# Routed expert blocks with eight row buffers and one plain slice; output weights prepared by GpSimd inside the attention core

## The reference

```
x = x + 0.5 * moe(layernorm(x))        # 16 experts, top 4 by sigmoid(x @ gate) + bias, plus a shared expert
x = x + attention(layernorm(x))        # 32 heads, 8 key/value heads of 16, rotary positions, causal
x = x + 0.5 * moe(layernorm(x))        # the same weights again
x = x + 0.5 * butterfly(layernorm(x))  # permuted features, 16 heads of 32 -> 128 -> 32, gelu
x = x + attention4(layernorm(x))       # 4 sequences, full attention at width 128
x = x + 0.5 * butterfly(layernorm(x))

moe:       zw_e = silu(x @ Wg_e.T) * (x @ Wu_e.T) * cw_e      # 256 columns each
           out  = sum over e of zw_e @ Wd_e.T
attention: out  = softmax(mask(q @ k.T / 16)) @ v @ w_dense.T + b_dense
```

## Time and profile before

| | us |
|---|---|
| median of three runs | 1367.78 (1367.69 to 1369.11) |
| the profiled execution | 1367.37 |
| its span, first to last instruction | 1365.6 |
| TensorE busy | 1144.0 (84%) |
| VectorE busy | 837.1 (61%) |
| ScalarE busy | 665.5 (49%) |
| GpSimd busy | 537.6 (39%) |
| mean granted TensorE clock | 0.905 of full speed |

### The profile page before, as it was taken

One profiled execution on the slowest core, in us unless ns is written; L12 is line 12 of the kernel. 1 busy time (PEld: TensorE's weight loads), 2 busy tenths in 40 slices (PEclk: granted clock), 3 DMA queues, 4 the chain that ended last, 5 costly groups with the idle time before them and its releaser, 6 DMA issues. The chain is left out here.

```text
span 1365.6 us, 22222 instructions
## 1 busy us (share of the span) xinstructions
PE 1144.0 (84%) x5800; PEld 723.2 (53%) x5801; DVE 837.1 (61%) x1527; ACT 665.5 (49%) x1218; POOL 537.6 (39%) x578
## 2 busy tenths in 40 slices
PE   5979999996284899999985796999999808777687
PEld 4747677674173344444424584676776605465454
DVE  4857777773455787777722565777777524445542
ACT  3136666663232277777772222666666503334133
POOL 4325555553673233333324324455555442050130
PEclk9979999998587699999998797999999957979879
DMA  9256989555405440000001454689955550010001
GB/s 349 100 203 156 241 238 248 100 104 90 183 35 133 95 89 2 1 1 1 1 1 39 181 189 170 179 206 264 253 107 100 81 167 0 4 37 0 20 12 62
DMA packets 63497, 151.64 MB, mean 111 GB/s; under 512 B 12560, under 2 KB 17488, under 8 KB 58832
## 3 DMA queue, kind: packets, MB, share of 16 engines
q1 hardware_dynamic: 40224, 99.83, 21.4%
q0 software_dynamic: 22592, 50.27, 19.4%
q10 hardware_dynamic: 624, 0.85, 0.4%
HBM read 105.75 MB, written 44.97 MB: 110 GB/s over the span
## 5 line engine op out<-in xcount | busy, mean ns | idle before, releaser
L715 POOL DMA_INDIRECT moe_acc_rows<-moe_out_rows,moe_token_of x94 | 165.4, 1760 | 196.5 <-ACT moe_out_rows L790 190.4
L1782 DVE TENSOR_REDUCE causal_top<-causal_mx 128x1 f32<-128x512 f32 (+3 forms) x384 | 192.0, 550 | 58.6 <-PE causal_mx L1634 50.5
L1746 ACT ACTIVATE causal_prob<-causal_sc 128x512 f32<-128x512 f32 (+3 forms) x384 | 169.9, 492 | 73.2 <-PE causal_sc L1652 70.7
L819 DVE TENSOR_TENSOR moe_w_lo<-moe_raw,moe_w_hi 128x1024 fp32r<-128x1024 f32 x94 | 115.1, 1225 | 112.7 <-ACT moe_w_hi L778 99.6
L730 PE MATMUL moe_gu<-moe_raw,moe_xt_plain 128*128 x376 | 180.5, 603 | 2.4 <-ACT moe_w_hi L778 2.4
L1631 PE MATMUL causal_mx<-causal_ks,causal_qs 96*128 (+4 forms) x384 | 130.9, 351 | 19.2 <-DMA causal_qs<-causal_parts 15.7
L778 ACT CAST moe_w_hi<-moe_raw 128x1024 fp32r x94 | 98.2, 1045 | 95.2 <-issue 90.8
L1652 PE MATMUL causal_sc<-causal_qs,causal_ks 99*128 (+3 forms) x384 | 123.7, 333 | 2.3 <-ACT causal_prob L1746 1.7
L708 POOL DMA_INDIRECT moe_rows<-moe_xn_rows,moe_token_of x94 | 93.3, 992 | 75.2 <-DVE moe_z L828 31.8
L822 DVE TENSOR_TENSOR moe_down_lo<-moe_raw,moe_down_hi 128x1024 fp32r<-128x1024 f32 x94 | 114.5, 1218 | 0.0
L735 PE MATMUL moe_gu<-moe_w_hi,xt_hi 128*128 128x512 f32 x188 | 112.7, 600 | 0.0
(11 more groups left out here) (273 smaller groups left out, 2425.0 us busy)
## 6 DMA issues: line engine op xcount, KB each, us to landing
moe_raw<-in_w_gu SPq DMA_DIRECT2D x34, 1024.0 KB
moe_raw<-in_w_down SPq DMA_DIRECT2D x34, 512.0 KB
causal_qs<-causal_parts SPq DMA_DIRECT2D x42, 128.0 KB, 3.3
moe_acc_rows<-moe_zeros SPq DMA_DIRECT2D x2, 2304.0 KB, 15.2
moe_acc_rows<-x SPq DMA_DIRECT2D x18, 256.0 KB, 2.0
moe_xn_rows<-xn SPq DMA_DIRECT2D x2, 2048.0 KB, 10.9
x<-moe_acc_rows SPq DMA_DIRECT2D x16, 256.0 KB, 5.3
xn<-moe_acc_rows SPq DMA_DIRECT2D x16, 256.0 KB, 5.9
```

Of the source, the lines that this page charges most:

```text
L715: pool.indirect_dma_start(acc_rows[a], bass.IndirectOffsetOnAxis(ap=token_of[:, b - 3:b - 2].bitcast(U32), axis=0), out_rows[(b - 3) % OUT ...
L819: nc.vector.tensor_tensor(w_lo[1 - s][:, :, :], raw[:, bass.ds(at + SPLIT_AT, GU_COLS - SPLIT_AT)].rearrange("p (k n) -> p k n", k=SPLIT), ...
L1746: nc.scalar.activation(prob[u % 2][:, h, o:CH], sc[(u * QPK + h) % BANKS][:, o:CH], ACT.Exp, scale=SCALE).then_inc(exp_done, 1)
L1782: nc.vector.tensor_reduce(top[:, kc, t, h:h + 1], mx[i % BANKS][:, 0:w], AX.X, ALU.max).then_inc(mx_read, 1)
```

## The change

Three things change in the routed blocks. RING becomes 8 and a new constant AHEAD = 6: the gather of block b+6 is issued in step b, once z of block b-2 is done (for the buffer that it reuses). PLAIN becomes 1, and so SPLIT 3. `out_rows` are slices of `xn`, which frees the space. The loop body of `run` thereby has eight steps.

In the causal attention layer the rounding and subtraction of `w_dense` and the addition of the bias move from the third part into the core, on GpSimd alone, one tile of each per group behind the mask of step 7; `w_dense` comes in two halves. The third part then has no loads and no GpSimd work, and TensorE alternates transposes and products.

```diff
-RING = 4
+RING = 8
+AHEAD = 6
-PLAIN = 2
+PLAIN = 1
 SPLIT = KT - PLAIN
...
-        out_rows = [sb(f"out_rows{s}", [P, H]) for s in range(OUTS)]
+        out_rows = [m.xn[:, s, :] for s in range(OUTS)]
...
-            for b in range(-3, NB + 3):
-                if there(b + 3):
-                    if b > 0:
-                        pool.wait_ge(z_done, b)
-                    pool.indirect_dma_start(rows[(b + 3) % RING][:, :], None, xn_rows, bass.IndirectOffsetOnAxis(
-                        ap=token_of[:, b + 3:b + 4].bitcast(U32), axis=0)).then_inc(gathered[(b + 3) % RING], 16)
+            for b in range(-AHEAD, NB + 3):
+                n = b + AHEAD
+                if there(n):
+                    if n >= RING:
+                        pool.wait_ge(z_done, n - RING + 1)
+                    pool.indirect_dma_start(rows[n % RING][:, :], None, xn_rows, bass.IndirectOffsetOnAxis(
+                        ap=token_of[:, n:n + 1].bitcast(U32), axis=0)).then_inc(gathered[n % RING], 16)
...
+            wd_hi = outer.enter_context(nc.sbuf_tensor(f"{name}_wd_hi", [P, KT, H], F32R))
+            wd_lo = outer.enter_context(nc.sbuf_tensor(f"{name}_wd_lo", [P, KT, H], F32R))
+            wd_raw = sb("wd_raw", [P, KT // 2, H])
+            b_out = sb("b_out", [P, H])
...
                         sp.dma_start(ks[a * HD:(a + 1) * HD, 0:S], parts_dram[K_PART[a], 0:HD, :]).then_inc(stack_in, 16)
+                    sp.dma_start(wd_raw[:, :, :], m.dram["w_dense"][:, 0:KT // 2, :]).then_inc(dense_in, 16)
+                    sp.dma_start(b_out[:, :], m.dram["b_dense"].rearrange("(a h) -> a h", a=1).broadcast_to([P, H])).then_inc(dense_in, 16)
                     with sp.Fori(1, KV) as g:
                         sp.wait_ge(stack_in, g * (16 * LOADS) - 16 * LOADS // 2)
                         load(g)
+                    sp.wait_ge(wd_ready, KT // 2)
+                    sp.dma_start(wd_raw[:, :, :], m.dram["w_dense"][:, KT // 2:KT, :]).then_inc(dense_in, 16)
...
+                    def prepare_dense(g):
+
+                        if g == 0:
+                            pool.wait_ge(dense_in, 32)
+                        if g == KT // 2:
+                            pool.wait_ge(dense_in, 48)
+                        if g < KT:
+                            raw = wd_raw[:, g % (KT // 2), :]
+                            nc.gpsimd.tensor_copy(wd_hi[:, g, :], raw).then_inc(wd_half, 1)
+                            pool.wait_ge(wd_half, g + 1)
+                            nc.gpsimd.tensor_tensor(wd_lo[:, g, :], raw, wd_hi[:, g, :].bitcast(F32),
+                                                    ALU.subtract).then_inc(wd_ready, 1)
+                        nc.gpsimd.tensor_tensor(m.x[:, g, :], m.x[:, g, :], b_out[:, :], ALU.add).then_inc(x_biased, 1)
+
...
+                            if u == C0 + 3:
+                                prepare_dense(g)
...
                 @block.tensor
                 def _(pe):
-                    for t in range(T):
-                        transpose_tile(m, pe, cm, xp[t % 2], t, ready=False)
-                    pe.wait_ge(wd_ready, 1)
-                    for t in range(T):
-                        pe.wait_ge(cm.xt_lo, t + 1)
-                        if t >= 2:
-                            pe.wait_ge(x_done, t - 1)
-                        rows = slice(t * P, (t + 1) * P)
-                        product(nc, yp[t % 2][:, :], [(m.xt_hi[:, k, rows], m.xt_lo[:, k, rows], wd_hi[:, k, :], wd_lo[:, k, :])
-                                                      for k in range(KT)]).then_inc(y_done, 1)
+                    pe.wait_ge(wd_ready, KT)
+                    for t in range(T + 1):
+                        if t < T:
+                            transpose_tile(m, pe, cm, xp[t % 2], t, ready=False)
+                        if t >= 1:
+                            pe.wait_ge(cm.xt_lo, t)
+                            if t >= 3:
+                                pe.wait_ge(x_done, t - 2)
+                            rows = slice((t - 1) * P, t * P)
+                            product(nc, yp[(t - 1) % 2][:, :], [(m.xt_hi[:, k, rows], m.xt_lo[:, k, rows], wd_hi[:, k, :],
+                                                                 wd_lo[:, k, :]) for k in range(KT)]).then_inc(y_done, 1)
...
                 @block.vector
                 def _(dve):
-                    for t in range(T):
-                        lo_tile(m, dve, cm, xp[t % 2], t)
-                    dve.wait_ge(x_biased, 1)
-                    for t in range(T):
+                    def finish(t):
                         dve.wait_ge(y_done, t + 1)
                         nc.vector.tensor_tensor(m.x[:, t, :], yp[t % 2][:, :], m.x[:, t, :], ALU.add).then_inc(x_done, 1)
                         next_stats(m, dve, x_done, t + 1, t)
 
+                    dve.wait_ge(x_biased, T)
+                    for t in range(T):
+                        lo_tile(m, dve, cm, xp[t % 2], t)
+                        if t >= 2:
+                            finish(t - 2)
+                    finish(T - 2)
+                    finish(T - 1)
```

More of the change, by code:

```diff
@@ L715, in _ @@
                     pool.indirect_dma_start(acc_rows[a], bass.IndirectOffsetOnAxis(ap=token_of[:, b - 3:b - 2].bitcast(U32), axis=0),
-                                            out_rows[(b - 3) % OUTS][:, :], None, compute_op=ALU.add).then_inc(scattered[a], 16)
+                                            out_rows[(b - 3) % OUTS], None, compute_op=ALU.add).then_inc(scattered[a], 16)
         @block.tensor
@@ L789, in step @@
                         act.wait_ge(scattered[a], (b - 1 - OUTS - a) * 8 + scattered_start[a])
-                    nc.scalar.copy(out_rows[(c - 3) % OUTS][:, :], y[1 - s][:, :]).then_inc(y_out, 1)
+                    nc.scalar.copy(out_rows[(c - 3) % OUTS], y[1 - s][:, :]).then_inc(y_out, 1)
                 if there(b):
@@ L1275, in causal_attention_layer @@
         ks = outer.enter_context(nc.sbuf_tensor(f"{name}_ks", [P, KV * S], BF16))
+        dense_in, wd_half, wd_ready, x_biased = sem("dense_in"), sem("wd_half"), sem("wd_ready"), sem("x_biased")
         with ExitStack() as ctx:
@@ L1830, in pb @@
                 return ctx.enter_context(nc.psum_tensor(f"{name}_{what}", shape, dt))
-            wd_raw = sb("wd_raw", [P, KT, H])
-            wd_hi = sb("wd_hi", [P, KT, H], F32R)
-            wd_lo = sb("wd_lo", [P, KT, H], F32R)
-            b_out = sb("b_out", [P, H])
             xp = [pb(f"xpd{s}", [P, CH]) for s in range(2)]
@@ L1838, in causal_attention_layer @@
             cm = NormSems(sem, "ctx")
-            wd_in, wd_half, wd_ready, x_biased, y_done, x_done = (
-                sem("wd_in"), sem("wd_half"), sem("wd_ready"), sem("x_biased"), sem("y_done"), sem("x_done"))
+            y_done, x_done = sem("y_done"), sem("x_done")
             with nc.Block() as block:
-                @block.sync
-                def _(sp):
-                    sp.dma_start(wd_raw[:, :, :], m.dram["w_dense"]).then_inc(wd_in, 16)
-                    sp.dma_start(b_out[:, :], m.dram["b_dense"].rearrange("(a h) -> a h", a=1).broadcast_to([P, H])).then_inc(wd_in, 16)
-                @block.gpsimd
-                def _(pool):
-                    pool.wait_ge(wd_half, 1)
-                    nc.gpsimd.tensor_tensor(wd_lo[:, :, :], wd_raw[:, :, :], wd_hi[:, :, :].bitcast(F32),
-                                            ALU.subtract).then_inc(wd_ready, 1)
-                    nc.gpsimd.tensor_tensor(m.x[:, :, :], m.x[:, :, :], b_out[:, :].unsqueeze(1).broadcast_to([P, T, H]),
-                                            ALU.add).then_inc(x_biased, 1)
@@ L1869, in _ @@
                 @block.scalar
                 def _(act):
-                    for t in range(2):
-                        hi_tile(m, act, cm, xp[t % 2], t)
-                    act.wait_ge(wd_in, 32)
-                    nc.scalar.copy(wd_hi[:, :, :], wd_raw[:, :, :]).then_inc(wd_half, 1)
-                    for t in range(2, T):
+                    for t in range(T):
                         hi_tile(m, act, cm, xp[t % 2], t)
```

## The result

The changed kernel took 1345.45 us, the median of four runs (1342.85 to 1349.18), beside 1367.9 for the kernel before (1367.69 to 1369.11). The ratio is 0.9836, 95% interval 0.9812 to 0.986: 22.4 us less. The forecast was 1343.5, the range 1337 to 1355. In a second session, later, the same kernel had 0.9822 (0.9802 to 0.9842).

A forecast was written before the change was run, and what follows sets the result against it. It took TensorE's matmuls to bound the routed phases, and GpSimd's preparation to hold up the output projection. 1367.4 - 14.4 - 10.5 + 1.0 = 1343.5 us, own range 1339 to 1348; the range with two rivals 1337 to 1355.

The forecast's parts named there:

- Plain slices: Routed blocks: one plain slice instead of two cuts the block period from 5.15 to 4.985 us, -14.4 us over two phases.
- The small terms: Start of each routed phase: longer w_hi and xt_hi +0.54, a slice saved at the lower clock -0.43, block 2's wait +0.3 us.
- Eight buffers: Routed blocks: gathers issued six blocks ahead change nothing, as steady state has no wait to remove; 0, ends -1.3 and +1.3 us.
- the three short waits: TensorE's waits for gathered rows beyond the two long ones: 12.9 - 2 x 5.8, gone or doubled, giving ends -1.3 and +1.3 us.
- Projection: Output projection: prepared weights and interleaved transposes shorten it from 40.9 us, ending at 755.8 instead of 766.3; -10.5 us.
- Preparation in the core: Attention core: GpSimd's added copy, subtraction and addition, 3.75 us, hide in its 4.71 us wait; cost 0, ends 0 and +1.6.
- Loads: Attention core's start: 512 KB of weights and 256 KB of bias share DMA engines with the first queries; +1.0 us, ends 0 and +3.
- ScalarE is not the bound: Rival, routed blocks: exposed register reads make ScalarE's loop 5.09 us, saving only 5.5 us in all; time 1352, chance 0.16.
- VectorE was never the bound: Rival, routed blocks: register reads exposed after zt_lo make VectorE's loop up to 5.56 us; time 1396, chance 0.07.
- The core was not slowed: Rival, attention core: VectorE stops for each new GpSimd operation, 20 us at most; time 1363.5, chance 0.07.
- the projection not kept slow: Rival, output projection: TensorE at the lower clock or a hand-over per tile, 5 us less saved; time 1348.5, chance 0.08.

## Why the prediction was right, and where it was not

- **Plain slices, -14.4.** The period came out at 4.99 (forecast 4.985); the two phases are 7.4 and 6.8 shorter in the first profile, 6.8 and 7.0 in the second (forecast 7.2). The small terms show too: block 2 waited 0.32 for w_lo, the first w_hi wait went from 1.3 to 1.6 (forecast +0.54). silu is late by nothing that grows.
- **Eight buffers, 0.** As the price of that edit alone it was low by some 3 us (1 to 5). "In steady state there is no wait to remove" rested on stretches that begin at 110 and 870 us and so leave out the 0.76 at 862.75; the three short waits are 1.5 us and not 1.3. As a statement about the kernel it was the step that failed: I looked for a wait that the buffers would remove, found none in steady state, and did not ask what held the gathers on time or what the other edit takes from that. The slices removed some 1.5 us of a distance that had none to spare: two periods of 0.16 less, out_rows 0.43 later on ScalarE and a scatter 0.54 longer make 1.3 of it. The -14.4 belongs to both edits together. The forecast held because the change contained both, which is luck: nothing in the working asked for the buffers. A kernel with the first alone would have been forecast at 1353 and measured 1369. The longer scatter was measured only after, but its rule could have been read before: all scatters beside down_lo ended some 1.46 behind its end, however early they began. But one row of TensorE's weight loads before, for 110 to 310 us, already said that rows sometimes arrive last in the middle of a phase; I had looked at the matmuls alone, which hide 0.2 us:

```profile
PEld moe_tx L744 <- DMA moe_rows<-moe_xn_rows,moe_token_of: 0.4, 2, 0.2
```

- **Projection, -10.5.** It was -9.5. The first product started at 2.56 behind the first transpose (forecast 2.55); the higher clock came 7.4 us after the stage's start and not 5.65 (granted clock 0.50 to 728 us, 0.94 from 728 to 730), so eleven passes of product 0 ran at the lower one, at 0.43 each from the second on, and not seven: 4 x 0.2 = 0.8. From there on a tile takes 3.235 (forecast 3.22).
- **Preparation in the core, 0.** GpSimd's operations took 0.61, 1.28 and 1.27, together 3.2 with their starts (forecast 3.75), and 1.58 of the wait is left. The copy was the overpriced one. The groups 1 to 6 are 32.34 against 32.36.
- **Loads, +1.0.** Four kernels without the preparation have their first maximum at 9.3, 8.3, 9.0 and 7.9 (mean 8.6); eight with it at 10.0 to 11.3 (mean 10.6): +2.0, inside the bounds.
- **Sum.** The stages give -7.4 - 6.8 - 9.5 + 1.5 = -22.2, the measured ratio -22.4. The profiled execution itself is only 18.2 shorter. The other 4 us lie in code that did not change (0.4 and 1.3 in the core, 0.7 ahead of phase 2, 1.9 behind it), and the same code takes 267.0 to 271.6 us behind phase 2 in other kernels of this study: one profile must not be read to the microsecond.
- **Rivals.** ScalarE is not the bound, but it has nothing left: with one split slice more, 0.54, it stretched the period. VectorE was never the bound. The core was not slowed beyond the later start, and the projection not kept slow.

## What to carry to other kernels

A transfer that nobody waits for may still be holding a zero margin. Before an edit shortens a loop, lay the distance between the issue of each prefetch and its use beside the longest landing and not the median, and list what is queued ahead of the issue on its own engine. Where two edits come together, price each with the other taken away.

## What the runs showed that I had not expected

- The issue of a gather on GpSimd took 0.99 us, also where w_lo started while it ran, but 2.56 where it began after w_lo (one gather of 72 in the changed kernel's middle stretches, 212.19 us); a scatter took 1.75 or 2.29 by where it met down_lo, 1.55 where it met neither. With no plain slice and four buffers scatters met w_lo instead and took 1.83 and 1.68; these too ended 1.47 and 1.46 behind its end.
- A gather of 128 rows landed 3.5 to 9.9 us after its issue, median 4.3 to 4.5 in most kernels and stretches; the long ones lay beside 1.5 MB weight loads.
- Idle time noted as issue before w_hi shrank from 1.03 us (90.8 in 88) to 0.85 (76.4 in 90) with one plain slice, and to 0.56 (45.8 in 82) with none and eight buffers: the fuller ScalarE is, the less of its register reads shows.
